# Expert loop of a two-layer gated network: rows marked three experts ahead, SiLU product kept in PSUM, low part of the down weight on VectorE

## The chip, the cores and the metric

One core of a Trainium2 chip. The metric is the device time of the whole program in microseconds (us); less is better. Before the change it is 2899.19 us, the median of three runs (2895.27 to 2901.91).

## What is computed

Four residual blocks run one after another on 1,024 tokens of width 512 (2 sequences of 512): a cross attention, a causal attention with a mixture of experts behind it, a second cross attention, and a quantised feed-forward. The change is in the mixture of experts of the second block, and nowhere else:

```python
logits = h @ wg                                   # 16 experts
topv, topi = jax.lax.top_k(logits, 4)             # 4 of them for each token
gate = jax.nn.softmax(topv, -1)
weights = jnp.zeros_like(logits).at[bidx, sidx, topi].set(gate)
a = silu(einsum('bsd,edh->bseh', h, w1)) * einsum('bsd,edh->bseh', h, w3)
y = einsum('bseh,ehd->bsed', a, w2)
moe = einsum('bsed,bse->bsd', y, weights)
return x + moe
```

w1, w3 and w2 (called gate, up and down weight here) are 512 x 512 for each expert.

## The kernel before

All matrix products of this stage are made of three products of fp32r halves: each operand is split in a high part (a copy to fp32r) and a low part (what the copy lost), and high x high, low x high and high x low are added up (`ACCURATE`). So each weight of 1 MB is loaded into one of two raw buffers `e_raw` by SP (L1751), copied to its high part by ACT (L1774, function `high`), and its low part is made by POOL as raw minus high (L1808, function `low`). The semaphore `s_lo` counts the low parts, three for each expert; SP's next load into a raw buffer waits for it.

The stage has two versions, chosen at run time by the count of the fullest expert. The one that runs here (functions `few_*`) gives each expert at most CAP = 320 tokens, in CT = 3 tiles of 128 places. The other (`every_*`) is compiled but not entered. For expert e, in the program's order on each engine:

- **PE** (`few_tensor`, L2142 on): gate and up product of the four chunks m of the hidden width, 24 matmuls of 320 columns each (L2154) into `GU[m % 2]`; then `order(e+2)`: 24 small matmuls (L2125) that multiply the marks of expert e+2 with the token table and so give the list of its tokens; then `turn(e+1)`: transposes of the gathered rows of the next expert (L2135), two chunks before and two behind the first tile of the down product; and the down product, 12 matmuls of 512 columns for each of three row tiles (L2172) into the two banks `Y`.
- **ACT** (`few_scalar`): high part of w2, which waits until the last down product of the expert before is done (there is one w2 buffer); per chunk SiLU (L1954) and `part_high` (L1943), the high part of the activation; high part of the next w1 behind chunk 1, of the next w3 behind chunk 3; then the high parts of the next expert's tokens (L1934).
- **DVE** (`few_vector`, L2084 on): per chunk the product of SiLU and up (L2095) into the SBUF buffer `act32`, then some of the marks (L2043), then `part_low` (L2089), the low part of the activation. Behind the chunks `targets` and `listed` (some small operations on the lists), the low parts of the next tokens (L2071), and the eviction of each row tile, scaled by the gate (L2104).
- **POOL** (`few_gpsimd`): gather of the rows of expert e+1 (three indirect DMAs, L1985), then the three scatter-adds of expert e-1 into `y_sum` (L1996), and between them the low parts of w2, of the next w1 and of the next w3. A scatter-add waits (`s_sum`) until the one before it has landed. Ahead of each of them stands a one-element operation (L1995, L1983).

A mark is a 128 x 384 comparison: for one tile of 128 tokens, which of the 384 places of the expert its token takes. There are eight for each expert, written into the single buffer `e_mine`, and `mark(e)` waits until `order(e-1)` has read it. Where they stand is set by two lines:

```python
MARKS = (0, 3, 6, NT, NT)                       # NT = 8
mark(e + 2, range(MARKS[m], MARKS[m + 1]))      # in chunk m, between product and part_low
```

PE's `order(e+2)` waits for all eight (`s_mine`). The first two experts are written out, the other fourteen are a loop over pairs.

Of the kernel before, what the change touches and what calls it, by code (L numbers as in the profile page):

```python
# [7 lines left out]
P = 128  # L8
BANK = 512
# [39 lines left out]
def program(nc, a, out):  # L49
    ctx = ExitStack()  # L50
    with ctx:
# [1158 lines left out]
        CAP = T * TOPK // NE * 5 // 4  # L1210
        CT = -(-CAP // P)
        PLACES = CT * P
        place = sb("m_place", [P, NE + 2, NT])
        crowded = sb("m_crowded", [P, 1], I32)
        moe = {}
        h_rows = nc.dram_tensor("h_rows", (T, D), F32, kind="Internal").ap()
# [490 lines left out]
        def experts():  # L1707
# [6 lines left out]
            w2 = [sb(f"e_w2{i}", [P, HC, D], F32R) for i in range(2)]  # L1714
            silu = [sb(f"e_silu{i}", [P, BANK]) for i in range(2)]
            act32 = [sb(f"e_act{i}", [P, BANK]) for i in range(2)]
            carry = sb("e_carry", [P, 2])
            aT0 = [sb(f"e_aT0{i}", [P, HC, BANK], F32R) for i in range(2)]
            with ExitStack() as every_only:
                aT = [aT0, [every_only.enter_context(nc.sbuf_tensor(f"e_aT1{i}", [P, HC, BANK], F32R)) for i in range(2)]]  # L1720
            with ExitStack() as few_only:
# [12 lines left out]
            s_in = [sem(f"e_in{i}") for i in range(2)]  # L1734
            s_mine, s_list, s_id, s_xt, s_xh, s_xl, s_got, s_tg = [
                sem(f"e_{n}") for n in ("mine", "list", "id", "xt", "xh", "xl", "got", "tg")]
            s_up = sem("e_up")
            s_freed = sem("e_freed")
            s_back = [sem(f"e_back{i}") for i in range(2)]
            s_sum = sem("e_sum")  # L1740
# [162 lines left out]
            def few_sync(sp):  # L1903
                def body(i, s, last):
                    e = i * 2 + s
                    for k, kind in enumerate(("w2", "w1", "w3")):
                        if not (last and k):
                            sp.wait_ge(s_lo, 3 * e + k + 1)
                            load(sp, 3 * s + k, e + (1 if k else 0), kind)

                sp.dma_start(count_up[:, :], a["c_count_up"].partition_broadcast(P)).then_inc(s_up, 16)
                load(sp, 0, 0, "w1")
                load(sp, 1, 0, "w3")
                with sp.Fori(0, NE // 2 - 1) as i:
                    for s in range(2):
                        body(i, s, False)
                body(NE // 2 - 1, 0, False)
                body(NE // 2 - 1, 1, True)
                sp.wait_ge(s_sum, 16 * CT * NE)
                for k in range(2):  # L1920
                    sp.dma_start(y3[:, k * NT // 2:(k + 1) * NT // 2, :],
                                 y_sum[k * T // 2:(k + 1) * T // 2, :].rearrange("(t p) d -> p t d", p=P)).then_inc(s_back[k], 16)

            def few_scalar(act):
# [13 lines left out]
                def body(i, s, last):  # L1938
                    e = i * 2 + s

                    def part_high(m):
                        act.wait_ge(s_a, HC * (e + 1) + m + 1)
                        act.activation(aT0[0][:, m, 0:CAP], act32[m % 2][:, 0:CAP], ACT.Copy).then_inc(s_ah, 1)  # L1943

                    def next_high(w, k):

                        n = 3 * s + k
                        high(act, w[1 - s][0], 16 * (3 * i + 1 + n // 2 + 1), n % 2)

                    act.wait_ge(s_y, CT * (e + 1))  # L1950
                    high(act, w2[0], 16 * (3 * i + (1 if s == 0 else 3)) + (0 if s else 16), s)
                    for m in range(HC):
                        act.wait_ge(s_gu, HC * (e + 1) + m + 1)
                        act.activation(silu[m % 2][:, 0:CAP], GU[m % 2][:, 0:CAP], ACT.Silu).then_inc(s_sg, 1)  # L1954
                        part_high(m)
                        if not last and m == 1:
                            next_high(w1, m)
                    if not last:
                        next_high(w3, 2)
                    tokens(e + 1, 1 - s)  # L1960
# [12 lines left out]
            def few_gpsimd(pool):  # L1973
# [3 lines left out]
                def gather(e, s):  # L1977

                    pool.wait_ge(s_id, LIST * e + LIST)
                    if not (isinstance(e, int) and e == 0):  # L1980
                        pool.wait_ge(s_xt, KC * e)

                    pool.tensor_tensor(carry[:, s:s + 1], eps[:, 0:1], eps[:, 0:1], ALU.mult)  # L1983
                    for r in range(CT):
                        pool.indirect_dma_start(rows[:, r, :], None, h_rows,  # L1985
                                                bass.IndirectOffsetOnAxis(ap=ids[s][:, r:r + 1], axis=0)).then_inc(s_got, 16)
# [17 lines left out]
                def body(i, s, first, last):  # L2004
                    e = i * 2 + s
                    gather(e + 1, 1 - s)
                    if not first:
                        scatter(e - 1, 1 - s, 0)
                    low(pool, w2, 3 * e + 3, s)
                    if not first:  # L2010
                        scatter(e - 1, 1 - s, 1)
                    if not last:
                        low(pool, w1[1 - s], 3 * e + 4, (3 * s + 1) % 2)
                    if not first:
                        scatter(e - 1, 1 - s, 2)
                    if not last:
                        low(pool, w3[1 - s], 3 * e + 5, (3 * s + 2) % 2)
# [12 lines left out]
            def few_vector(dve):  # L2030
# [48 lines left out]
                listed(1, 1)  # L2079
                tokens(0, 0)  # L2080

                MARKS = (0, 3, 6, NT, NT)

                def body(i, s):  # L2084
                    e = i * 2 + s

                    def part_low(m):
                        dve.wait_ge(s_ah, HC * e + m + 1)
                        dve.tensor_tensor(aT0[1][:, m, 0:CAP], act32[m % 2][:, 0:CAP], aT0[0][:, m, 0:CAP].bitcast(F32),  # L2089
                                          ALU.subtract).then_inc(s_al, 1)  # L2090

                    for m in range(HC):
                        dve.wait_ge(s_al, HC * e + m + 1)
                        dve.wait_ge(s_sg, HC * e + m + 1)
                        dve.tensor_tensor(act32[m % 2][:, 0:CAP], silu[m % 2][:, 0:CAP], GU[m % 2][:, BANK:BANK + CAP],  # L2095
                                          ALU.mult).then_inc(s_a, 1)
                        mark(e + 2, range(MARKS[m], MARKS[m + 1]))
                        part_low(m)
                    targets(e, s)
                    listed(e + 2, s)  # L2100
# [1 line left out]
                    for r in range(CT):  # L2102
                        dve.wait_ge(s_y, CT * (e + 1) + r + 1)
                        dve.tensor_scalar(y3[:, CT * s + r, :], Y[(r + 1) % 2][:, :], share[s][:, r:r + 1], None, ALU.mult).then_inc(s_yd, 1)  # L2104

                for s in range(2):
                    body(0, s)
# [5 lines left out]
            def few_tensor(pe):  # L2113
# [28 lines left out]

                def body(i, s):
                    e = i * 2 + s
                    pe.wait_ge(s_lo, 3 * e + 1)
                    pe.wait_ge(s_xl, KC * (e + 1))
                    for m in range(HC):
                        pe.wait_ge(s_a, HC * (e + 1) + m - 1)
                        for j, w in enumerate((w1[s], w3[s])):
                            if j and m == 0:  # L2150
                                pe.wait_ge(s_lo, 3 * e + 2)
                            for n, (x0, x1) in enumerate(ACCURATE):
                                for c in range(KC):
                                    mm = pe.matmul(GU[m % 2][:, j * BANK:j * BANK + CAP], w[x0][:, c, m * P:(m + 1) * P],  # L2154
# [4 lines left out]
                    order(e + 2)  # L2159

                    turn(e + 1, range(2))
                    pe.wait_ge(s_lo, 3 * e + 3)
                    pe.wait_ge(s_al, HC * (e + 1) + 1)
                    for r in range(CT):
                        pe.wait_ge(s_yd, CT * (e + 1) + max(r - 1, 0))
# [851 lines left out]
```

## Time and profile before

| | |
|---|---|
| median of 3 runs | 2899.19 us (2895.27 to 2901.91) |
| profiled execution, its own time | 2897.7 us |
| its span | 2895.9 us |
| PE busy | 2411.6 us (83%) |
| DVE busy | 1781.1 us (62%) |
| ACT busy | 1482.8 us (51%) |
| POOL busy | 1160.3 us (40%) |
| granted PE clock, mean | 0.934 |
| gate and up products (L2154), PE busy | 230.4 us |
| low parts of weights (L1808), POOL busy | 222.0 us for 48, 4627 ns each |

The expert stage runs from about 1708 to 2200 us of the span. Shares are of the span of one profiled execution; a granted clock of 1 is 2.4 GHz and 0.5 is 1.2 GHz. Operations are named by line, engine and the tiles that they write and read.

### The profile page before, as it was taken

The page shows a single profiled execution, that of the slowest core. Times are in us where ns is not written, and L with a number is a line of the kernel's source. Part 1 is how long each engine was busy: PE and PEld are TensorE (multiplying, and loading weights), DVE is VectorE, ACT ScalarE, POOL GpSimd, SP SyncE. Part 2 cuts the span into 40 slices and gives each one's busy share as a digit, 9 for nine tenths or more (in the row PEclk, how much of TensorE's full clock was granted, in tenths as well). Part 3 has the DMA queues.
Part 4 walks back from the last instruction along what each step waited for, and adds up shares of the span by engine and source line. Part 5 has one row for each costly group of instructions (what it writes and reads, how often), then busy time and mean ns, then how long its engine had stood idle before and what let it go on. Part 6 is the DMA issues. An engine that isn't in the chain of part 4 may idle for free. (4 is left out here: it accounts for less than half of the span.)

```text
span 2895.9 us, 46257 instructions
## 1 busy us (share of the span) xinstructions
PE 2411.6 (83%) x14790; PEld 2004.4 (69%) x14790; DVE 1781.1 (62%) x3865; ACT 1482.8 (51%) x3037; POOL 1160.3 (40%) x1561
## 2 busy tenths in 40 slices
PE   6999999999975998889885749999994698899365
PEld 3778787878864888888874538888883576677232
DVE  2555555555544666666665626565655787788576
ACT  3444444444435666666663443344332776777543
POOL 0222222222222444444442467787771544444000
PEclk9999999999996999999996969999997899999778
DMA  3000000000001000000003465665556332321100
GB/s 110 19 12 18 7 18 11 14 11 18 0 1 40 19 19 18 18 18 18 8 11 122 156 227 151 174 167 165 162 148 167 90 93 63 95 76 66 76 8 22
DMA packets 123653, 190.90 MB, mean 66 GB/s; under 512 B 18273, under 2 KB 66657, under 8 KB 121761
## 3 DMA queue, kind: packets, MB, share of 16 engines
q1 hardware_dynamic: 111408, 161.69, 18.3%
q0 software_dynamic: 10992, 25.96, 4.0%
q10 hardware_dynamic: 1152, 2.10, 0.3%
q8 instruction: 41, 0.67, 0.1%
q14 instruction: 60, 0.48, 0.1%
HBM read 143.58 MB, written 46.14 MB: 66 GB/s over the span
## 5 line engine op out<-in xcount | busy, mean ns | idle before, releaser
L435 ACT ACTIVATE x_p<-x_p,x_least 128x1024 f32<-128x1024 f32 x128 | 147.3, 1151 | 307.5 <-DVE x_least L391 307.5
L1808 POOL TENSOR_TENSOR e_w<-e_raw,e_w 128x2048 fp32r<-128x2048 f32 x48 | 222.0, 4627 | 70.5 <-ACT e_w L1774 70.4
L469 POOL TENSOR_TENSOR x_carry<-x_rtotal 128x1 f32<-128x1 f32 x128 | 24.7, 193 | 560.0 <-DVE x_rtotal L368 560.0
L375 DVE TENSOR_TENSOR x_pT<-pair,x_pT 128x512 fp32r<-128x512 f32 x256 | 164.4, 684 | 122.4 <-ACT x_pT L454 122.4
L2154 PE MATMUL pair<-m_h,e_w 128*128 128x320 f32 x1536 | 230.4, 311 | 1.1 <-DVE m_h L2071 1.1
L2154 PEld LDWEIGHTS pair<-m_h,e_w 128*128 128x128 f32 x1536 | 229.0, 190 | 2.9 <-issue 1.5
L537 PE MATMUL pair<-x_pT,x_v 128*128 128x256 f32 x1536 | 209.6, 293 | 9.2 <-DVE x_pT L375 9.2
L537 PEld LDWEIGHTS pair<-x_pT,x_v 128*128 128x128 f32 x1536 | 194.0, 194 | 26.3 <-issue 18.3
L565 PE MATMUL pair<-x_kT,x_qT 128*128 128x512 f32 x768 | 207.1, 405 | 0.0
L993 ACT ACTIVATE s_p<-s_p,s_least 128x128 f32<-128x128 f32 (+3 forms) x256 | 143.6, 561 | 123.4 <-DVE s_least L903 123.4
L2497 DVE TENSOR_REDUCE z_most<-pair 128x1 f32<-128x1008 f32 x128 | 154.0, 1203 | 73.4 <-PE pair L2607 51.2
L1131 PE MATMUL pair<-s_pT,s_v 128*128 128x256 f32 (+1 forms) x1152 | 158.3, 284 | 47.6 <-DVE s_pT L880 47.6
L1131 PEld LDWEIGHTS pair<-s_pT,s_v 128*128 128x128 f32 x1152 | 152.7, 195 | 60.1 <-issue 30.8
L2519 ACT ACTIVATE z_pT<-pair 128x512 fp32r<-128x512 f32 x256 | 141.7, 601 | 95.7 <-PE pair L2568 82.8
L1053 POOL TENSOR_TENSOR s_carry<-s_rtotal 128x1 f32<-128x1 f32 x256 | 49.6, 194 | 346.8 <-DVE s_rtotal L874 346.5
L2568 PE MATMUL pair<-ident,z_p 128*128 128x128 f32 x1024 | 144.6, 281 | 51.0 <-DVE z_pT L2490 49.9
L2533 ACT ACTIVATE z_p<-pair,z_most 128x1008 f32<-128x1008 f32 (+1 forms) x256 | 174.3, 696 | 12.5 <-DVE z_most L2498 12.5
L2568 PEld LDWEIGHTS pair<-ident,z_p 128*128 128x128 f32 x1024 | 117.1, 142 | 90.4 <-DVE z_pT L2490 61.8
L880 DVE TENSOR_TENSOR s_pT<-pair,s_pT 128x128 fp32r<-128x128 f32 (+3 forms) x256 | 124.7, 487 | 81.1 <-ACT s_pT L979 81.1
L2553 POOL TENSOR_SCALAR z_p<-z_p,z_rtotal 128x1008 f32<-128x1008 f32 (+1 forms) x256 | 174.6, 695 | 0.0
L2490 DVE TENSOR_TENSOR z_pT<-pair,z_pT 128x512 fp32r<-128x512 f32 x256 | 163.1, 679 | 4.5 <-ACT z_pT L2519 3.8
L454 ACT ACTIVATE x_pT<-pair 128x512 fp32r<-128x512 f32 x256 | 138.3, 594 | 45.0 <-PE pair L523 45.0
(336 smaller groups left out, 6189.9 us busy)
## 6 DMA issues: line engine op xcount, KB each, us to landing
e_raw<-in_L_ffn_w SPq DMA_DIRECT2D x48, 1024.0 KB
z_v<-z_vst SPq DMA_DIRECT2D x16, 768.0 KB, 3.6
z_kS<-z_k SPq DMA_DIRECT2D x24, 512.0 KB, 10.6
z_vS<-z_v SPq DMA_DIRECT2D x8, 1536.0 KB, 6.5
f_raw<-in_L_ffn_w SPq DMA_DIRECT2D x2, 4096.0 KB, 13.4
z_qS<-z_q SPq DMA_DIRECT2D x24, 256.0 KB, 4.5
s_wraw<-in_L_ffn_wq SPq DMA_DIRECT2D x9, 512.0 KB, 4.4
x_wq<-in_L_xattn_Wq SPq DMA_DIRECT2D x8, 512.0 KB, 3.6
```

The costliest lines, as they stand in the source:

```text
L375: dve.tensor_tensor(pT[1][:, keys, q * P:(q + 1) * P], TR[j][:, :].rearrange("p (k n) -> p k n", n=P), pT[0][:, keys, q * P:(q + 1) * P].b ...
L435: act.activation(p[n][:, :], p[n][:, :], ACT.Exp, scale=-1.0, bias=least[:, n:n + 1], accum_out=total[:, n:n + 1]).then_inc(s_ex, 1)
L537: mm = pe.matmul(OB[:, cols], v[x0][b][:, k, :], pT[x1][:, k, cols], start=(half == 0 and n == 0 and k == 0), stop=(half == 1 and n == 2 a ...
L565: mm = pe.matmul(SC[n % 2][:, j * BANK:(j + 1) * BANK], qT[x0][b][n // QT][:, n % QT * P:(n % QT + 1) * P], kT[x1][b][:, j * BANK:(j + 1) ...
L1131: mm = pe.matmul(OB[:, cols], v[b][:, k, first:first + 2, :].rearrange("p k d -> p (k d)"), pT[x1][:, k, cols], start=(i % 2 == 0 and half ...
L1808: pool.tensor_tensor(dst[1][:, :, :], raw[parity][:, :, :], dst[0][:, :, :].bitcast(F32), ALU.subtract).then_inc(s_lo, 1)
L2154: mm = pe.matmul(GU[m % 2][:, j * BANK:j * BANK + CAP], w[x0][:, c, m * P:(m + 1) * P], XS[s][x1][:, c, :], start=(n == 0 and c == 0), sto ...
L2490: dve.tensor_tensor(pT[1][:, k, cols], TR[i][:, :].rearrange("p (k n) -> p k n", n=P), pT[0][:, k, cols].bitcast(F32), ALU.subtract).then_ ...
L2497: dve.tensor_reduce(most[:, w, 0:1], SC[n % 2][:, 0:MAIN], AX.X, ALU.max, negate=True)
L2533: act.activation(p[w][:, cols], SC[n % 2][:, cols], ACT.Exp, bias=most[:, w, k:k + 1], accum_out=total[:, w, k:k + 1]).then_inc(s_ex, 1)
L2553: pool.tensor_scalar(p[w][:, cols], p[w][:, cols], rtotal[:, w, k:k + 1], 1.0, ALU.mult, ALU.mult).then_inc(s_pn, 1)
L2568: mm = pe.transpose(TR[i][:, k * P:(k + 1) * P], p[n % RING][:, kk * P:(kk + 1) * P], ident[:, :])
```

## The change

It does three things, all in the `few_*` functions.

1. **Marks.** They leave the four chunks. `mark(e+3)` now stands behind the row evictions of expert e, three behind the first, three behind the second and two behind the third; `mark(2)` is made whole ahead of the first expert. `place` gets one more column of zeros for it.
2. **Product.** The product of SiLU and up is written back into `GU` (PSUM) over the gate half, and `part_high` and `part_low` read it there. PE's wait ahead of a chunk is now for `part_low` of the chunk two before (`s_al`), where it was for the product (`s_a`).
3. **Low part of w2.** It moves from POOL to DVE, to the head of an expert's work, with a semaphore of its own (`s_lo2`). On POOL the first two scatter-adds then stand next to each other.

```diff
@@ -1210,7 +1210,7 @@
         CAP = T * TOPK // NE * 5 // 4
         CT = -(-CAP // P)
         PLACES = CT * P
-        place = sb("m_place", [P, NE + 2, NT])
+        place = sb("m_place", [P, NE + 3, NT])
         crowded = sb("m_crowded", [P, 1], I32)
         moe = {}
         h_rows = nc.dram_tensor("h_rows", (T, D), F32, kind="Internal").ap()
@@ -1714,7 +1714,6 @@
             w2 = [sb(f"e_w2{i}", [P, HC, D], F32R) for i in range(2)]
             silu = [sb(f"e_silu{i}", [P, BANK]) for i in range(2)]
             act32 = [sb(f"e_act{i}", [P, BANK]) for i in range(2)]
-            carry = sb("e_carry", [P, 2])
             aT0 = [sb(f"e_aT0{i}", [P, HC, BANK], F32R) for i in range(2)]
             with ExitStack() as every_only:
                 aT = [aT0, [every_only.enter_context(nc.sbuf_tensor(f"e_aT1{i}", [P, HC, BANK], F32R)) for i in range(2)]]
@@ -1734,7 +1733,7 @@
             s_in = [sem(f"e_in{i}") for i in range(2)]
             s_mine, s_list, s_id, s_xt, s_xh, s_xl, s_got, s_tg = [
                 sem(f"e_{n}") for n in ("mine", "list", "id", "xt", "xh", "xl", "got", "tg")]
-            s_up = sem("e_up")
+            s_up, s_lo2 = sem("e_up"), sem("e_lo2")
             s_freed = sem("e_freed")
             s_back = [sem(f"e_back{i}") for i in range(2)]
             s_sum = sem("e_sum")
@@ -1905,7 +1904,10 @@
                     e = i * 2 + s
                     for k, kind in enumerate(("w2", "w1", "w3")):
                         if not (last and k):
-                            sp.wait_ge(s_lo, 3 * e + k + 1)
+                            if k < 2:
+                                sp.wait_ge(s_lo, 2 * e + k + 1)
+                            else:
+                                sp.wait_ge(s_lo2, e + 1)
                             load(sp, 3 * s + k, e + (1 if k else 0), kind)
 
                 sp.dma_start(count_up[:, :], a["c_count_up"].partition_broadcast(P)).then_inc(s_up, 16)
@@ -1940,7 +1942,7 @@
 
                     def part_high(m):
                         act.wait_ge(s_a, HC * (e + 1) + m + 1)
-                        act.activation(aT0[0][:, m, 0:CAP], act32[m % 2][:, 0:CAP], ACT.Copy).then_inc(s_ah, 1)
+                        act.activation(aT0[0][:, m, 0:CAP], GU[m % 2][:, 0:CAP], ACT.Copy).then_inc(s_ah, 1)
 
                     def next_high(w, k):
 
@@ -1980,7 +1982,7 @@
                     if not (isinstance(e, int) and e == 0):
                         pool.wait_ge(s_xt, KC * e)
 
-                    pool.tensor_tensor(carry[:, s:s + 1], eps[:, 0:1], eps[:, 0:1], ALU.mult)
+                    pool.tensor_tensor(scrap[:, 58 + s:59 + s], eps[:, 0:1], eps[:, 0:1], ALU.mult)
                     for r in range(CT):
                         pool.indirect_dma_start(rows[:, r, :], None, h_rows,
                                                 bass.IndirectOffsetOnAxis(ap=ids[s][:, r:r + 1], axis=0)).then_inc(s_got, 16)
@@ -2006,7 +2008,6 @@
                     gather(e + 1, 1 - s)
                     if not first:
                         scatter(e - 1, 1 - s, 0)
-                    low(pool, w2, 3 * e + 3, s)
                     if not first:
                         scatter(e - 1, 1 - s, 1)
                     if not last:
@@ -2079,22 +2080,23 @@
                 listed(1, 1)
                 tokens(0, 0)
 
-                MARKS = (0, 3, 6, NT, NT)
+                MARKS = (0, 3, 6, NT)
+                mark(2)
 
                 def body(i, s):
                     e = i * 2 + s
+                    dve.wait_ge(s_hi, 3 * e + 3)
+                    dve.tensor_tensor(w2[1][:, :, :], raw[s][:, :, :], w2[0][:, :, :].bitcast(F32), ALU.subtract).then_inc(s_lo2, 1)
 
                     def part_low(m):
                         dve.wait_ge(s_ah, HC * e + m + 1)
-                        dve.tensor_tensor(aT0[1][:, m, 0:CAP], act32[m % 2][:, 0:CAP], aT0[0][:, m, 0:CAP].bitcast(F32),
+                        dve.tensor_tensor(aT0[1][:, m, 0:CAP], GU[m % 2][:, 0:CAP], aT0[0][:, m, 0:CAP].bitcast(F32),
                                           ALU.subtract).then_inc(s_al, 1)
 
                     for m in range(HC):
-                        dve.wait_ge(s_al, HC * e + m + 1)
                         dve.wait_ge(s_sg, HC * e + m + 1)
-                        dve.tensor_tensor(act32[m % 2][:, 0:CAP], silu[m % 2][:, 0:CAP], GU[m % 2][:, BANK:BANK + CAP],
+                        dve.tensor_tensor(GU[m % 2][:, 0:CAP], silu[m % 2][:, 0:CAP], GU[m % 2][:, BANK:BANK + CAP],
                                           ALU.mult).then_inc(s_a, 1)
-                        mark(e + 2, range(MARKS[m], MARKS[m + 1]))
                         part_low(m)
                     targets(e, s)
                     listed(e + 2, s)
@@ -2102,6 +2104,7 @@
                     for r in range(CT):
                         dve.wait_ge(s_y, CT * (e + 1) + r + 1)
                         dve.tensor_scalar(y3[:, CT * s + r, :], Y[(r + 1) % 2][:, :], share[s][:, r:r + 1], None, ALU.mult).then_inc(s_yd, 1)
+                        mark(e + 3, range(MARKS[r], MARKS[r + 1]))
 
                 for s in range(2):
                     body(0, s)
@@ -2142,13 +2145,13 @@
 
                 def body(i, s):
                     e = i * 2 + s
-                    pe.wait_ge(s_lo, 3 * e + 1)
+                    pe.wait_ge(s_lo, 2 * e + 1)
                     pe.wait_ge(s_xl, KC * (e + 1))
                     for m in range(HC):
-                        pe.wait_ge(s_a, HC * (e + 1) + m - 1)
+                        pe.wait_ge(s_al, HC * e + m + 1)
                         for j, w in enumerate((w1[s], w3[s])):
                             if j and m == 0:
-                                pe.wait_ge(s_lo, 3 * e + 2)
+                                pe.wait_ge(s_lo, 2 * e + 2)
                             for n, (x0, x1) in enumerate(ACCURATE):
                                 for c in range(KC):
                                     mm = pe.matmul(GU[m % 2][:, j * BANK:j * BANK + CAP], w[x0][:, c, m * P:(m + 1) * P],
@@ -2159,7 +2162,7 @@
                     order(e + 2)
 
                     turn(e + 1, range(2))
-                    pe.wait_ge(s_lo, 3 * e + 3)
+                    pe.wait_ge(s_lo2, e + 1)
                     pe.wait_ge(s_al, HC * (e + 1) + 1)
                     for r in range(CT):
                         pe.wait_ge(s_yd, CT * (e + 1) + max(r - 1, 0))
```

On DVE, from the evictions of expert 0 into the chunks of expert 1 (written-out part; `y` is the evicted tile, `e_mine` the marks, `e_act` the product in SBUF, `e_aT` the low part of the activation). Before:

```order
L2104 TENSOR_SCALAR y<-pair,e_share 128x512 x3
L2095 TENSOR_TENSOR e_act<-e_silu,pair 128x320
L2043 TENSOR_SCALAR e_mine<-e_count_up,m_place 128x384 x3
L2089 TENSOR_TENSOR e_aT<-e_act,e_aT 128x320
L2095 TENSOR_TENSOR e_act<-e_silu,pair 128x320
L2043 TENSOR_SCALAR e_mine<-e_count_up,m_place 128x384 x3
L2089 TENSOR_TENSOR e_aT<-e_act,e_aT 128x320
L2095 TENSOR_TENSOR e_act<-e_silu,pair 128x320
L2043 TENSOR_SCALAR e_mine<-e_count_up,m_place 128x384 x2
L2089 TENSOR_TENSOR e_aT<-e_act,e_aT 128x320
```

and now (line numbers of the changed kernel):

```order
L2106 TENSOR_SCALAR y<-pair,e_share 128x512
L2044 TENSOR_SCALAR e_mine<-e_count_up,m_place 128x384 x3
L2106 TENSOR_SCALAR y<-pair,e_share 128x512
L2044 TENSOR_SCALAR e_mine<-e_count_up,m_place 128x384 x3
L2106 TENSOR_SCALAR y<-pair,e_share 128x512
L2044 TENSOR_SCALAR e_mine<-e_count_up,m_place 128x384 x2
L2089 TENSOR_TENSOR e_w<-e_raw,e_w 128x2048
L2098 TENSOR_TENSOR pair<-e_silu,pair 128x320
L2093 TENSOR_TENSOR e_aT<-pair,e_aT 128x320
L2098 TENSOR_TENSOR pair<-e_silu,pair 128x320
L2093 TENSOR_TENSOR e_aT<-pair,e_aT 128x320
```

The marks have gone from between the products to between the evictions, and one operation of 2,048 columns stands ahead of the first product.

On POOL, the work of expert 1 (`y_sum<-y` is a scatter-add, `e_rows` the gather, `e_w` a low part). Before:

```order
L1985 DMA e_rows<-h_rows,e_ids 128x512 x3
L1995 TENSOR_TENSOR scrap<-eps 128x1
L1996 DMA y_sum<-y,e_target 1408x512
L1808 TENSOR_TENSOR e_w<-e_raw,e_w 128x2048
L1995 TENSOR_TENSOR scrap<-eps 128x1
L1996 DMA y_sum<-y,e_target 1408x512
L1808 TENSOR_TENSOR e_w<-e_raw,e_w 128x2048
L1995 TENSOR_TENSOR scrap<-eps 128x1
L1996 DMA y_sum<-y,e_target 1408x512
L1808 TENSOR_TENSOR e_w<-e_raw,e_w 128x2048
```

and now:

```order
L1987 DMA e_rows<-h_rows,e_ids 128x512 x3
L1997 TENSOR_TENSOR scrap<-eps 128x1
L1998 DMA y_sum<-y,e_target 1408x512
L1997 TENSOR_TENSOR scrap<-eps 128x1
L1998 DMA y_sum<-y,e_target 1408x512
L1807 TENSOR_TENSOR e_w<-e_raw,e_w 128x2048
L1997 TENSOR_TENSOR scrap<-eps 128x1
L1998 DMA y_sum<-y,e_target 1408x512
L1807 TENSOR_TENSOR e_w<-e_raw,e_w 128x2048
```

One of three low parts has left, the one between the first and the second scatter-add.

## Rows read from the trace of the kernel before

**Rows 1.** Stretches: PE, PEld, DVE, ACT, POOL busy; clock, DMA share, GB/s.

```profile
1960.80:1989.57 28.77, 26.74 (x170) 24.40 (x168) 16.79 (x32) 10.47 (x15) 22.37 (x14) 0.94 0.59 163
2102.47:2129.72 27.25, 25.33 (x169) 23.16 (x168) 16.62 (x32) 10.63 (x16) 21.25 (x12) 1.00 0.58 153
2157.33:2182.00 24.67, 24.67 (x170) 22.54 (x168) 13.34 (x33) 6.98 (x13) 12.42 (x10) 1.00 0.40 60
1730.69:2157.33 426.64, 395.33 (x2520) 360.53 (x2521) 251.66 (x479) 167.09 (x240) 335.62 (x194) 0.96 0.59 166
```

**Rows 2.** The chain of waits around experts 14 and 15: start, length, what.

```profile
2144.50 1.16 issue
...
2146.23 1.49 PE pair L2125 x24
...
2151.23 0.66 PE pair L2135 x6
2151.88 5.61 PE pair L2172 x24
2157.49 14.08 PE pair L2154 x96
2171.58 0.60 PE pair L2125 x24
2172.17 0.72 PE pair L2135 x6
2172.89 2.81 PE pair L2172 x12
```

**Rows 3.** The timeline of the expert that PE begins at 1961.03 us.

```profile
1961.34 1.92 ACT L1774 ACTIVATE e_w<-e_raw 128x2048 fp32r<-128x2048 f32 x1 [3.76 <-PE pair L2172]
...
1972.03 4.57 POOL L1808 TENSOR_TENSOR e_w<-e_raw,e_w 128x2048 fp32r<-128x2048 f32 x1 [1.99 <-ACT e_w L1774]
...
1972.77 4.38 DVE L2043 TENSOR_SCALAR e_mine<-e_count_up,m_place 128x384 bf16<-128x384 f32 x2
...
1978.36 1.90 ACT L1774 ACTIVATE e_w<-e_raw 128x2048 fp32r<-128x2048 f32 x1
...
1980.61 0.89 DVE L2071 TENSOR_TENSOR m_h<-pair,m_h 128x320 fp32r<-128x320 f32 x2 [0.38 <-ACT m_h L1934]
...
1984.90 0.18 POOL L1983 TENSOR_TENSOR e_carry<-eps 128x1 f32<-128x1 f32 x1
...
1988.82 0.21 POOL L1995 TENSOR_TENSOR scrap<-eps 128x1 f32<-128x1 f32 x1
```

**Rows 4.** The marks' own line: shortest, median and longest in ns.

```profile
L2043 DVE TENSOR_SCALAR e_mine<-e_count_up,m_place x144: 405/410/4057, 1713.3 to 2169.4; 128x384 bf16<-128x384 f32 x144
```

**Rows 5.** PE behind a wait for marks: stretch, busy (matmuls), granted clock, DMA share, GB/s.

```profile
1948.00:1955.00 7.00, 6.58 (x45) 0.76 0.71 187
```

**Rows 6.** The one DVE line elsewhere with the shape and form of the moved operation.

```profile
L1377 DVE TENSOR_TENSOR z_cT<-z_ctxraw,z_cT x2: 2285/2288/2291, 1574.1 to 1576.3; 128x2048 fp32r<-128x2048 f32 x2
```

**Rows 7.** The products' line on DVE: shortest, median and longest in ns.

```profile
L2095 DVE TENSOR_TENSOR e_act<-e_silu,pair x64: 473/486/490, 1737.4 to 2172.2; 128x320 f32<-128x320 f32 x64
```

**Rows 8.** The scatter-adds' line on POOL, and their time to landing.

```profile
L1996 POOL DMA_INDIRECT y_sum<-y,e_target x48: 1562/1621/1681, 1762.4 to 2189.6; - x48
...
DMA to landing us min/median/max: 4.5/6.4/8.0
```

**Rows 9.** The timeline ahead of the first expert.

```profile
1717.28 2.71 DVE L2043 TENSOR_SCALAR e_mine<-e_count_up,m_place 128x384 bf16<-128x384 f32 x8
...
1718.34 1.77 POOL L1985 DMA_INDIRECT e_rows<-h_rows,e_ids  x1 [0.60 <-issue]
1720.42 0.97 POOL L1985 DMA_INDIRECT e_rows<-h_rows,e_ids  x1 [0.30 <-issue]
```

**Rows 10.** The chain at the head of the first expert, and behind the last.

```profile
1730.69 6.17 PE pair L2154 x24
...
2178.51 4.74 DMA y_sum<-y,e_target
```

## The prediction

> **What bounds the kernel now.** I read the busy shares first, then the chain of waits, then the expert stage by stretches and its timeline. In the expert stage PE works nearly all the time. The first fifteen experts take 426.64 us, 28.44 each, and PE is busy for 395.33 of them: 31.3 us idle, 2.09 for each expert [rows 1]. Read single: 28.77 us with 26.74 busy, 27.25 with 25.33 busy, and the last expert 24.67 without a gap [rows 1]. The chain names the gap: behind the last gate and up product it goes over DVE's marks (1.16 us of issue, a mark) to the small matmuls of `order`, which take 1.49 us there and 0.60 in the last expert [rows 2]. The reader is to see two things in that pair of rows. PE stands in front of marks that are not ready. And when it doesn't stand, the same 24 matmuls take 0.89 us less: I read this as their address registers, which are then set while earlier matmuls still run.
>
> Why the marks are late: one takes 0.41 us in the median and up to 4.06 [rows 4]. POOL begins a low part at 1972.03 and ends it at 1976.60; the pair of marks begins at 1972.77 and is over at 1977.15, so the first stood until POOL was through [rows 3]. `part_low`, the fourth product and all behind them queue after it on DVE. The last expert has no next weights, POOL makes no low part in its later chunks, and there is no gap: it is the picture of the changed kernel, inside the old one.
>
> A third cost hangs on the gap: the granted clock. Over 7 us behind one wait it is 0.76 [rows 5], so some 3.4 us at the lower level, 1.2 GHz, where the expert at 27.25 us shows 1.00 throughout [rows 1]. What went before is a PE idle of about 2 us. It explains most of the 1.5 us between the two kinds of expert.
>
> **The change, part by part.**
>
> *Marks to the evictions.* This removes the wait (2.09), the slow `order` (0.89) and, if the clock holds, the drops. The pieces of an expert without them are 14.08 gate and up, 0.60 order, 0.72 and 0.66 transposes, 2.81 and 5.61 down product [rows 2]: 24.48 us. Against 28.44 that is 3.96, of which 2.98 are the first two terms and 0.98 the clock, 0.18 of it the slow head of the first expert (24 matmuls in 6.17 us [rows 10], for a quarter of 14.08 = 3.52), which stays. At their new place the marks meet POOL's low part of w3. That begins when ACT has made the high part, about 3.4 us behind the last gate product, 17.5 from PE's start, and takes 4.57 [rows 3]: until 22.1. The first eviction is over at 14.1+0.6+0.7+2.8+0.75 = 19.0, so its three marks stand until 22.1 and end about 23.2, and the second eviction comes 1.3 us late. Nobody on the path waits for it: the third tile needs the first eviction, the list the second one 16 us later. All eight marks are over about 1.5 us into the next expert. Cost nothing; cover gone, each eviction held up costs PE what it is late. The eight extra marks ahead of the first expert take 2.7 us [rows 9] beside PE's 6.17 [rows 10]; nothing.
>
> The Trainium skill (SBUF — State Buffer, "Who interferes with whom") has the rule behind this: a DVE operation in a two-port mode and a GpSimd operation exclude each other for the whole instruction. The trace agrees with the 4.06 us above. By that rule the new place is no safer than the old one, only less waited for.
>
> *Tokens.* With the gap gone a shorter one may open. Behind the last gate product SiLU, product and high part end at about 1.6 us; ACT then makes w3's high part (1.90), and DVE's token parts begin 2.25 behind its start [rows 3], at 3.75, the first ready at 4.2. PE wants it at 0.60+0.72+2.81 = 4.13 [rows 2]. Bounds 0.1 and 0.5; I take 0.35 for each expert.
>
> *Product in PSUM.* No row shows DVE writing PSUM. Below, it costs what the write to SBUF costs, 0.486 [rows 7]; above, twice that, which would delay the tokens by 0.49 and cost 7 us in all. Reading it from PSUM is priced by the token parts, two in 0.89 [rows 3], as now. I take nothing more: both are one pass over 320 columns. PE's new wait, for `part_low` two chunks back, has cover: see next.
>
> *Low part of w2 on DVE.* The same form took 2.29 [rows 6]. The high part ends 2.2 us into the expert [rows 3], so DVE is busy to 4.6. SiLU of chunk 0 is ready at 4.1; the product moves to 5.1, `part_low` ends at 6.3, and PE wants it at 7.05 (two quarters of 14.08). 0.8 us of cover, then each us more is paid once per expert. SP's load of the next w3 starts 2.3 us sooner, as the raw buffer comes free sooner.
>
> *POOL.* It loses 4.6 us per expert but also the work that hid the landing of the first scatter-add. Its own round is now gather 3.92 [rows 3], three one-element operations of 0.4, two landings L, the third issue 1.62 [rows 8], and the low part of w3 4.6; w1's hides in the second landing. That is 11.3 + 2L: 20.3, 24.1 or 27.3 us for L of 4.5, 6.4 or 8.0 [rows 8]. PE's round is 24.83. The likeliest value leaves PE the bound, by 0.7.
>
> **The sum.** 15 x (24.48 + 0.35) + 2.65 = 375.1 us for 426.6, so 51.5 less; the last expert and what follows, three scatter-adds landing one after another (4.74 for one [rows 10]), stay. The profiled execution takes 2897.7, and the median is 1.5 above it: 2899.2 - 51.5 = **2847.7 us**.
>
> **The rivals.**
> (a) *POOL's round becomes the bound.* For it: descriptors made beside marks took 1.77 us, where the next took 0.97 [rows 9], and marks now run beside the gather, so up to two of three issues may grow by 0.8 and the round reaches 25.7 at L = 6.4; the loads come closer together, too. Then 15 x 0.9 = 13 us more: 2861. The same page of the Trainium skill says that a GpSimd-queue DMA starves for descriptors while DVE is in such a mode; by that rule this case is the likelier. Against it: DVE's marks stand behind the low part for part of that time. With L at 8.0 it is 27.3, 37 us more: 2885.
> (b) *DVE is late at the head of the expert* (w2's low part behind held marks, or slower): 2 us of delay less 0.8 of cover is 1.2 x 15 = 18 us: 2866. Against it: the marks end 0.8 us before the high part does.
> (c) *The change doesn't do all it says*: the clock falls without the gap as well. Then 0.8 x 15 = 12 us more: 2860.
> (d) *Slower than before.* POOL's chain of landings, the first scatter-add now bare, exceeds 28.44 us. It decides at L = 8.6. At 9.0 it is 29.3: 13 us slower than before, 2912. Against it: the longest of 48 landings took 8.0 [rows 8].
>
> **How the numbers follow.** Forecast 0.65, (a) small 0.13 and large 0.04, (b) 0.06, (c) 0.07, (d) 0.03, and 0.02 for a gain that comes out at nothing for a reason not seen. The forecast's own bounds are 24.58 per expert (2844) and, with the dear PSUM write, 25.3 (2855); the three runs reach 3.9 us below their median, and that goes below: 2840. (a) small, (b) and (c) reach to 2866, so the range is 2840 to 2867 and leaves out the large (a), (d) and the ends. Faster by over 0.2%, about what a measurement of this kernel can tell from none: 0.65+0.13+0.04+0.06+0.07 = 0.95; within 0.2%: 0.02; slower: 0.03.
>
> **What would show it.** Right: experts 24.6 to 25.1 us apart, `order` at 0.60 us, no PE wait for marks, clock 1.00 from the second expert on, marks up to about 3.5 us long behind the first eviction. Wrong: PE waiting for `e_w` or for rows (POOL's round), `part_low` late for the third chunk (DVE), or half-clock stretches without a gap ahead of them. The forecast falls if POOL is found without idle time and the experts are over 25.3 us apart.

## The result, and the profile after

The changed kernel takes **2845.32 us** (median of 5 runs, 2844.33 to 2848.66) for 2899.28 of the kernel before, run on the same chip: a ratio of 0.9814, 95% interval 0.9803 to 0.9825, 54 us less. Forecast were 2847.7 us and a range of 2840 to 2867. The profiled execution took 2844.89 us, its span is 2843.1.

Stretches of the changed kernel; columns as in [rows 1]: experts 1 to 14, the last one, and one of the fourteen.

```profile
1756.96:2102.86 345.90, 343.19 (x2354) 316.15 (x2354) 206.64 (x462) 155.31 (x223) 248.20 (x169) 1.00 0.71 191
2102.86:2127.20 24.34, 24.34 (x169) 22.47 (x168) 13.86 (x33) 6.84 (x13) 8.24 (x10) 1.00 0.42 66
1979.33:2004.04 24.71, 24.54 (x171) 22.59 (x170) 14.79 (x33) 10.44 (x15) 17.73 (x13) 1.00 0.70 188
```

Fourteen experts in 345.90 us are 24.71 each, PE idle for 0.19 of them, the clock at 1.00: it answers to the row of fifteen experts in [rows 1] (28.44, idle 2.09, clock 0.96). From PE's first matmul of expert 0 (1729.82) to that of expert 15 (2102.86) it is 373.0 us for 426.6, so 53.6 us less; the two profiled executions differ by 52.8 (2897.7 and 2844.9). The rest of the program adds up to 0.8 us more: 0.9 less ahead of the loop, 1.7 more from expert 15 on.

The chain of waits of the changed kernel through one expert:

```profile
1979.33 14.11 PE pair L2157 x96
...
1993.47 0.45 ACT e_silu L1956
1993.94 0.51 DVE pair L2098
...
1994.80 1.91 ACT e_w L1773
1996.70 0.33 ACT m_h L1936
1997.06 0.50 DVE m_h L2072
...
1997.70 0.85 PE pair L2138 x6
1998.55 5.49 PE pair L2175 x24
2004.04 14.11 PE pair L2157 x96
```

No mark is in it. In the kernel before every expert of the loop has one on the chain, between the rows of [rows 2] this one:

```profile
2145.66 0.42 DVE e_mine L2043
```

The reader is to see what took their place: behind the last gate product the chain leaves PE for the last product, then w3's high part (1.91 us) and the next tokens, and comes back to PE's transposes at 1997.70, 0.17 us after PE had run dry. This is the short token wait that was expected.

The timeline of the same expert:

```profile
1981.43 2.29 DVE L2089 TENSOR_TENSOR e_w<-e_raw,e_w 128x2048 fp32r<-128x2048 f32 x1 [0.55 <-ACT e_w L1773]
...
1986.03 0.18 POOL L1997 TENSOR_TENSOR scrap<-eps 128x1 f32<-128x1 f32 x1 [3.32 <-DMA y_sum<-y,e_target]
...
1993.27 0.76 PE L2128 MATMUL pair<-e_token,e_mine 128*128 x24
...
1996.79 4.61 POOL L1807 TENSOR_TENSOR e_w<-e_raw,e_w 128x2048 fp32r<-128x2048 f32 x1 [0.57 <-ACT e_w L1773]
...
1999.53 0.74 DVE L2106 TENSOR_SCALAR y<-pair,e_share 128x512 f32<-128x512 f32 x1
2000.19 2.09 DVE L2044 TENSOR_SCALAR e_mine<-e_count_up,m_place 128x384 bf16<-128x384 f32 x3
```

`order` begins with the end of the gate products (x24 in 0.76; the timeline counts its overlap with them, the chain has 0.60 for such a group). The moved low part takes 2.29 us, as its like in [rows 6]. POOL waits 3.3 us for the first scatter-add to land, 47.8 us in all fourteen experts. All of it is slack, as a run below shows. The marks behind the first eviction are still held by POOL's low part (1996.79 to 2001.40) and go on when it ends.

The marks, the product written to PSUM, and the landings, to be laid beside [rows 4], [rows 7] and [rows 8]:

```profile
L2044 DVE TENSOR_SCALAR e_mine<-e_count_up,m_place x152: 401/410/1529, 1712.5 to 2128.2; 128x384 bf16<-128x384 f32 x152
```

```profile
L2098 DVE TENSOR_TENSOR pair<-e_silu,pair x64: 487/495/497, 1736.3 to 2117.5; 128x320 f32<-128x320 f32 x64
```

```profile
DMA to landing us min/median/max: 4.6/5.3/7.1
```

The longest mark takes 1.53 us, where it took 4.06; a product costs 0.01 us more for going to PSUM; a landing takes 5.3 us in the median, not 6.4.

### The profile page after: what moved, and what is told of

It reads as the page before. It is cut to its first block and busy times, and to the rows that moved or that the text cites. A ratio compares the mean times of both kernels' runs of the same rounds, so it can differ in the third digit from the quotient of the medians.

```text
span 2843.1 us, 46195 instructions
## 1 busy us (share of the span) xinstructions
PE 2385.3 (84%) x14782; PEld 1985.4 (70%) x14790; DVE 1755.0 (62%) x3889; ACT 1482.6 (52%) x3037; POOL 1086.3 (38%) x1545
## 5 line engine op out<-in xcount | busy, mean ns | idle before, releaser
L1807 POOL TENSOR_TENSOR e_w<-e_raw,e_w 128x2048 fp32r<-128x2048 f32 x32 | 146.7, 4587 | 39.6 <-ACT e_w L1773 39.6
```

Source lines behind the costliest of these rows:

```text
L1807: pool.tensor_tensor(dst[1][:, :, :], raw[parity][:, :, :], dst[0][:, :, :].bitcast(F32), ALU.subtract).then_inc(s_lo, 1)
```

## The experiments

Ten more kernels ran. The distance of experts is that of experts 1 to 14, from PE's first matmul of one to that of the next; idle is PE's per expert; both come from a stretch as above. The time of the kernel before on the same chip stands beside each.

| run | median us | before | ratio (95%) | expert | idle | clock |
|---|---|---|---|---|---|---|
| before | | | 1 | 28.16 | 2.09 | 0.97 |
| the change | 2845.3 | 2899.3 | 0.9814 (0.9803 to 0.9825) | 24.71 | 0.19 | 1.00 |
| marks only | 2868.1 | 2902.2 | 0.9883 (0.9867 to 0.9900) | 26.10 | 1.37 | 1.00 |
| marks and PSUM product | 2850.0 | 2902.2 | 0.9821 (0.9805 to 0.9838) | 24.71 | 0.19 | 1.00 |
| marks and low part on DVE | 2855.5 | 2902.2 | 0.9841 (0.9824 to 0.9857) | 25.50 | 0.75 | 1.00 |
| all but the marks | 2902.6 | 2902.2 | 1.0002 (0.9992 to 1.0012) | 28.42 | 1.60 | 0.93 |
| before, other table | 2883.4 | 2900.8 | 0.9937 (0.9920 to 0.9953) | 27.19 | 2.01 | 0.99 |
| all but the marks, other table | 2844.7 | 2900.8 | 0.9808 (0.9791 to 0.9824) | 24.71 | 0.19 | 1.00 |
| the change, a wait put in | 2916.6 | 2899.6 | 1.0062 (1.0046 to 1.0077) | 29.12 | 2.71 | 0.95 |
| the same, fixed address | 2888.5 | 2899.6 | 0.9962 (0.9946 to 0.9977) | 27.29 | 2.13 | 0.97 |
| the change, free scatter-adds | 2839.6 | 2899.6 | 0.9798 (0.9785 to 0.9811) | 24.70 | 0.19 | 1.00 |
| the same, tokens first | 2832.2 | 2899.6 | 0.9769 (0.9755 to 0.9782) | 24.31 | 0.00 | 1.00 |

### Which part brings the gain

**Marks only.** The changed kernel with the product in `act32` and w2's low part on POOL, both as before. The cut shows where each went; the two readers of the product and the waits that belong to it are set back too.

```diff
-                    dve.wait_ge(s_hi, 3 * e + 3)
-                    dve.tensor_tensor(w2[1][:, :, :], raw[s][:, :, :], w2[0][:, :, :].bitcast(F32), ALU.subtract).then_inc(s_lo2, 1)
...
+                    pool.wait_ge(s_hi, 3 * e + 3)
+                    pool.tensor_tensor(w2[1][:, :, :], raw[s][:, :, :], w2[0][:, :, :].bitcast(F32), ALU.subtract).then_inc(s_lo2, 1)
...
-                        dve.tensor_tensor(GU[m % 2][:, 0:CAP], silu[m % 2][:, 0:CAP], GU[m % 2][:, BANK:BANK + CAP],
+                        dve.tensor_tensor(act32[m % 2][:, 0:CAP], silu[m % 2][:, 0:CAP], GU[m % 2][:, BANK:BANK + CAP],
```

> The changed kernel with its other two parts undone: the product goes to SBUF again and w2's low part is on POOL again; only the marks have moved. My theory: PE's wait for the marks goes, but part_low, a DVE operation with two SBUF inputs, is shut out by POOL's low parts, which the marks took the blame for before: part_low of chunks 0 and 2 ends with POOL's operation, the fourth product and the tokens come 1 to 2 us late and PE waits for the tokens; experts 25.5 to 27 us apart, 2858 to 2880 us. Rival 1 (the marks are everything): experts 24.7 us apart, 2845 us. Rival 2 (POOL's round with three low parts is the bound without the slack of the wait): PE waits for e_w, over 2880 us.

Measured: 2868.1 us, experts 26.10 apart, both inside what the theory said. The timeline around the third chunk shows why:

```profile
1930.62 4.57 POOL L1807 TENSOR_TENSOR e_w<-e_raw,e_w 128x2048 fp32r<-128x2048 f32 x1 [1.02 <-ACT e_w L1773]
...
1931.98 3.56 DVE L2093 TENSOR_TENSOR e_aT<-e_act,e_aT 128x320 fp32r<-128x320 f32 x1 [0.54 <-ACT e_aT L1945]
...
1935.46 0.47 DVE L2099 TENSOR_TENSOR e_act<-e_silu,pair 128x320 f32<-128x320 f32 x1
```

`part_low`, 0.49 us when free, begins at 1931.98 and ends at 1935.54, just behind POOL's operation (1935.19). The next product stands behind it on DVE. PE waits twice in each expert: 0.76 us at the down product, which needs this `part_low`, and 0.61 for the tokens. It never waits for `e_w`. Rivals 1 and 2 fall: it isn't all in the marks, and POOL is not the bound.

**Marks and PSUM product**: the first two lines of the diff above undone on DVE, put on POOL; the product stays in PSUM.

> Marks moved and product in PSUM, but w2's low part on POOL as before. My theory: part_low has one SBUF input now and is never shut out, and POOL's round of some 23.7 us fits under 24.7, so this is as fast as the whole change: 2845 us, within 3 us. Rival (the low part on DVE is what is needed, since POOL has no room for it): POOL without idle time, experts 25 to 26 us apart, 2850 to 2865 us.

Measured: experts 24.71 apart, ratio 0.9821, inside the interval of the whole change. The 2850.0 us are 2 above the range that was expected; this chip gives the kernel before 2902.2. `part_low` in this run, and in the run with the marks only:

```profile
L2093 DVE TENSOR_TENSOR e_aT<-pair,e_aT x64: 491/492/493, 1743.3 to 2124.5; 128x320 fp32r<-128x320 f32 x64
```

```profile
L2093 DVE TENSOR_TENSOR e_aT<-e_act,e_aT x64: 491/494/3572, 1742.6 to 2144.0; 128x320 fp32r<-128x320 f32 x64
```

The longest is 0.493 us with one input in PSUM and 3.57 with both in SBUF; POOL makes its three low parts for each expert in both.

**Marks and low part on DVE**: the product in SBUF again (last pair of the diff).

> Marks moved and w2's low part on DVE, but the product in SBUF as before. My theory: part_low of chunk 2 meets POOL's low part of w1 and ends with it, about 3 us late; the fourth product and the tokens follow 0.5 to 1.5 us late; experts 25.2 to 26.2 us apart, 2853 to 2868 us. Rival (an operation with two SBUF inputs is not shut out): part_low stays at 0.49 us each and the time is 2845 us.

Measured: experts 25.50 us apart, 2855.5 us in all, ratio 0.9841, as expected. That is 0.79 us per expert behind the change: `part_low` still meets w1's low part (3.30 us at the longest). So with the marks gone, the PSUM product is what frees DVE; moving w2's low part then adds nothing that shows, and without the PSUM product it is worth 0.60 us per expert (26.10 to 25.50).

**All but the marks**: `mark(e + 2, ...)` back in the chunks with the table (0, 3, 6, NT, NT), the rest of the change in place.

> The marks back in the chunks, two experts ahead, with the product in PSUM and w2's low part on DVE. My theory: the last marks still meet POOL's low part of w1 and PE waits for them as before; at most the first chunk's marks get through sooner: 2885 to 2900 us. Rival (POOL's third low part was what held the marks, so moving it alone brings the gain): PE's wait goes, 2850 to 2865 us.

Measured: 2902.6 us, ratio 1.0002. That is slower than the 2885 to 2900 expected: the theory was right that the wait would stay, and wrong that something would be gained. The rival falls. Its chain has the old wait:

```profile
1947.43 0.45 ACT e_silu L1956
...
1948.30 4.07 DVE e_mine L2044 x2
...
1952.51 1.48 PE pair L2127 x24
```

PE's idle time fell from 2.09 to 1.60 us per expert, but its busy time rose from 26.07 to 26.81, with the granted clock at 0.93 for 0.97. That gave it back.

### Is it the place of the marks, or what they meet there?

**Before, other table**: one line of the kernel before.

```diff
-                MARKS = (0, 3, 6, NT, NT)
+                MARKS = (0, 4, NT, NT, NT)
```

> The kernel before with one line changed: the numbers that place the marks are (0, 4, 8, 8, 8), so that four stand in chunk 0, four in chunk 1 and none in chunk 2. My theory: what held the last marks was POOL's low part of w1, which begins behind chunk 1; the ones in chunk 1 are then made ahead of it, PE's wait for marks goes, and part_low of chunk 2 (two SBUF inputs) stands behind that low part in their place, as in the run where only the marks were moved: experts 25.8 to 26.6 us apart, ratio 0.985 to 0.991, 2860 to 2872 us. Rival (marks between the products cost PE a wait wherever they stand): experts 28 us apart or more, ratio 0.998 to 1.005.

Measured: 0.9937, between the theories' ranges: a miss. The wait for marks is gone, as the theory has it. But the four marks in chunk 0 are now held by POOL's low part of w2 (4.51 us; four unheld ones take 1.40), and `part_low` of chunk 2 by that of w1. Two places of the timeline:

```profile
1957.55 4.51 DVE L2043 TENSOR_SCALAR e_mine<-e_count_up,m_place 128x384 bf16<-128x384 f32 x4
```

```profile
1965.27 4.54 POOL L1808 TENSOR_TENSOR e_w<-e_raw,e_w 128x2048 fp32r<-128x2048 f32 x1 [2.40 <-ACT e_w L1774]
1966.69 3.47 DVE L2089 TENSOR_TENSOR e_aT<-e_act,e_aT 128x320 fp32r<-128x320 f32 x1 [0.61 <-ACT e_aT L1943]
...
1970.26 3.04 PE L2172 MATMUL pair<-e_w,e_aT 128*128 128x512 f32 x12 [1.82 <-POOL e_w L1808]
```

The down product waits 1.8 us. The profile names POOL's operation, but that was over at 1969.81; what the program waits for there is this `part_low`, over at 1970.16. The expectation had left out the first of the two: behind the held marks chunk 1 is late, with it ACT's high part of w1 and POOL's low part, and so `part_low` of chunk 2 ends later. The down product waits 1.57 us per expert for it, 0.76 in the run with the marks only.

**All but the marks, other table**: the same line in the kernel of 1.0002.

> The same table in the kernel that has the marks in the chunks, the product in PSUM and w2's low part on DVE (without the table 1.000 of the time before). My theory: no mark and no part_low meets a low part of POOL; part_low of chunk 0 comes at about 7.0 us where PE wants it at 7.05, so there may be a small wait there: experts 24.7 to 25.2 us apart, ratio 0.981 to 0.984. Rival (marks must leave the chunks): over 0.99.

Measured: 0.9808, experts 24.71 apart, no mark longer than 0.64 us. So the marks need not leave the chunks. What they must not meet is POOL's low parts; with w2's on DVE, chunks 0 and 1 are free of them. This table was not run with w2's low part left on POOL and the product in PSUM.

### What a wait on PE costs

**The change, a wait put in**, and **the same, fixed address**. The first cut is in both, the second in the latter alone; it gives the loop's experts the shares of expert 2, so its output is not the layer's, while the amount of work is the same.

```diff
                     pe.wait_ge(s_yd, CT * (e + 1) - 1)
+                    pe.wait_ge(s_al, HC * (e + 1) + 2)
                     order(e + 2)
```

```diff
-                            tok = moe["token"][:, e, t, :] if isinstance(e, int) else (
-                                moe["token"][:, bass.ds(e, 1), t, :].rearrange("p e k -> p (e k)"))
+                            tok = moe["token"][:, e if isinstance(e, int) else 2, t, :]
```

> The changed kernel with one wait more on PE: ahead of order it waits for the low part of the fourth chunk (about 2.1 us behind the last gate product), which it would wait for later anyway. My theory: the wait of about 2.1 us in 16 experts brings with it the slow order (1.49 for 0.60 us) and half-clock stretches, less 0.3 us of token wait that it swallows: 3.3 to 3.6 us per expert, 2895 to 2905 us. Rival (the wait alone costs, the other two terms are something else): 1.8 us per expert, 2874 us.

> As the run with the added wait, but order inside the loop reads the token table at a fixed expert (2), so that its 24 matmuls need no address register; the shares of the loop's experts are then those of expert 2, the amount of work is the same. If the slow order is its registers being set behind the wait: order takes 0.6 to 0.8 us and the time is 10 to 14 us below the run with the wait alone. If it is an effect of the idle time or the clock on the matmuls: order stays near 1.49 us and the time is the same.

Measured: 2916.6 and 2888.5 us. The chain behind the wait, first with the address in a register, then with the fixed one:

```profile
1949.34 0.45 ACT e_silu L1956
...
1951.55 1.53 PE pair L2128 x24
1953.08 1.38 PE pair L2138 x6
1954.46 4.88 PE pair L2176 x12
```

```profile
1942.47 0.50 DVE e_aT L2093
...
1943.10 0.75 PE pair L2127 x24
1943.85 0.71 PE pair L2137 x6
1944.56 2.77 PE pair L2175 x12
```

With a fixed address `order` takes 0.75 to 0.80 us behind the same wait in all sixteen experts, with the register 1.45 to 1.53. The rows of the address registers show when they are set, in the run with the wait and in the changed kernel:

```profile
L2128 PEldq FUSED_REGOPS  x8: 46/46/51, 1951.4 to 1952.4; - x8
L2128 PEldq FUSED_REGOPS  x8: 46/46/65, 1990.8 to 1991.8; - x8
```

Behind the wait the eight are set from just ahead of the first matmul of `order` to past its middle (it runs from 1951.55 to 1953.08). Without the wait they are done 1.4 us before `order` begins (1993.27), and with the fixed address there are none. The clock is not the reason: in the kernel before `order` takes 1.46 to 1.49 us in the ten experts where its stretch has clock 1.00, and 1.48 to 1.52 in the five at 0.55 to 0.87. What is left between 0.76 and 0.60 I read as lost overlap: the timeline above shows 0.76 for an `order` without a wait too, and the chain counts 0.60 of it because it begins beside the last gate products.

Both expectations were too low in size. The wait costs 4.41 us per expert (29.12 for 24.71), not 3.3 to 3.6: idle 2.52 more, `order` 0.9 more, and about 1 us from stretches at a lower clock (0.95 in the mean), as the down product's 4.88 for 2.77, with 0.54 granted. The fixed address saves 28 us, not 10 to 14: 1.83 per expert, of which 0.72 are `order` (1.49 and 0.77 in the mean), 0.58 less idle, and the rest goes with the clock (0.97 for 0.95). How these hang together was not taken apart.

### What is left

**The change, free scatter-adds**:

```diff
-                    if not (isinstance(e, int) and e == 0 and r == 0):
-                        pool.wait_ge(s_sum, 16 * (CT * e + r))
+                    if r == 0 and not (isinstance(e, int) and e == 0):
+                        pool.wait_ge(s_sum, 16 * CT * e)
```

> The changed kernel, with the wait ahead of a scatter-add only at the first of an expert's three: the three write different rows (a token is once in an expert's list), so only those of the expert before must have landed. Behind the last expert the three were 5.5 us apart, each behind the landing of the one before; now about 2 us: 6 to 7 us less, 2838 to 2840 us. In the loop POOL gains slack, worth nothing if PE is the bound, as I hold. If POOL's round bounds in part (rival a of the prediction), the experts also come closer together than 24.71 us.

Measured: 2839.6 us, as expected, with experts 24.70 apart: only the end of the stage got shorter. From PE's start on expert 15 to the reload of `y_sum` it is 30.3 us for 36.7 (2103.77 to 2134.08, and 2102.86 to 2139.58). That the experts don't come closer shows POOL's round not to be the bound.

**The same, tokens first**: on ACT and on DVE `tokens(e + 1, 1 - s, range(2))` stands ahead of `next_high(w3, 2)` and of `targets`, the other two chunks where all four were.

> As the run without the waits between an expert's scatter-adds, and the first two chunks of the next tokens are made on ACT ahead of w3's high part and on DVE ahead of the small list operations. If the token wait (0.23 us over the pieces, 24.71 for 24.48) is the last one of PE: experts 24.45 to 24.5 us apart, 3 to 4 us below the other run, 2835 us. If w3's high part, now 0.9 us later, pushes POOL or the loads: no gain or a loss of up to 5 us.

Measured: 2832.2 us, the fastest of all, 0.9769. It is 7.4 us below the other run, not 3 to 4, and the experts are 24.31 apart, not 24.45 to 24.5: the pieces that the expectation subtracted from were 0.17 us too long. The chain through one expert is PE alone:

```profile
1952.85 14.10 PE pair L2159 x96
1966.94 0.60 PE pair L2130 x24
1967.54 0.71 PE pair L2140 x6
1968.26 2.79 PE pair L2177 x12
1971.05 0.66 PE pair L2140 x6
1971.70 5.46 PE pair L2177 x24
```

340.35 us busy in 340.35: 24.31 per expert. PE has no idle time left there and its clock is at 1.00, so only less work on PE would bring the experts closer.

## Why the prediction was right, point by point

- **The wait for marks, the slow `order`, the clock.** Right in kind and size for the change as a whole: idle 2.09 to 0.19, `order` 0.60 us, clock 1.00 from the second expert on. But the prediction gives all of it to the moving of the marks. Alone that brought 2.06 of the 3.45 us per expert, and 34 of the 54 us. That the slow `order` is its registers was read from one pair of rows; the fixed address showed it for 0.72 of the 0.89 us. That a wait brings stretches at a lower clock was shown by putting one in.
- **The undisturbed expert**, 24.48 us by its pieces: it is 24.31. The down products are a little shorter than in [rows 2] (5.46 and 2.79 for 5.61 and 2.81); why, stays open. **The token wait**, 0.35 taken: 24.71 less 24.31 is 0.40. Of this 0.19 is idle time, and as much is the transposes' lost overlap (0.85 for 0.66). The two errors partly cancel: 24.71 for 24.83, some 2 us in all, by which the forecast was high.
- **Marks at their new place.** Right that they are held by w3's low part and that it costs nothing. The step that timed them was wrong: it put the first eviction's end at 19.0 us behind PE's start, by the down product alone. On DVE the low parts of the third and fourth token chunk stand ahead of it, and it ends about 2 us later (2000.27 less 1979.33), so the marks are held less (2.09 us for the three, not 4; the longest is 1.53, not 3.5).
- **Product in PSUM.** Right that it adds next to nothing (0.01 us each), and wrong on what it is worth. The part on it priced only its own cost; that `part_low` would be held in the marks' place was not seen. It is this edit that keeps `part_low` out of POOL's way; without it 0.79 us per expert are lost, and 1.39 with w2's low part on POOL. The Trainium skill (SBUF — State Buffer, "Who interferes with whom") states this for a DVE operation with two SBUF inputs against a GpSimd operation that reads SBUF; the prediction used the rule for the marks and not for `part_low`. Here the runs agree with it: 3.57 us for 0.49 with both inputs in SBUF, 0.493 at most with one. The sum came out because the edit was in the change all the same: to that extent the hit is luck.
- **Low part of w2 on DVE.** 2.29 us, ends 4.4 us behind PE's start; right, and it was worth nothing by itself beside the PSUM product.
- **POOL's round** (rival a, and the decision point of rival d). A landing took 5.3 us, so the round is 11.3 + 10.6 = 21.9 us, and the runs without the waits left the experts where they were. The premise that issues beside marks are drawn out did not hold in the loop: beside them (1978.45, marks from 1978.15 on) an issue took 0.99 us, and none of the gather's took over 1.03.
- **Rivals b and c** did not come: `part_low` had its cover, and the clock did not fall once the gap was gone.

## What to carry to other kernels

When PE waits for a small operation, look at what that one meets on GpSimd before moving it: here a table of two numbers, with one operand kept in PSUM and w2's low part on DVE, did as much as moving the marks out of the chunks. A PE wait of 2 to 2.5 us in each round cost 3.5 to 4.4: the address registers were set behind it (0.9 us), and the clock was lower in part of what followed. And when one wait goes, work out which is next: it was the 0.40 us for the tokens, and a change of order on two engines took that as well.

## What was not expected of the hardware

- With the marks in their old place, the product in PSUM and w2's low part on DVE shortened PE's idle time from 2.09 to 1.60 us and came with a lower mean clock, 0.93 for 0.97; the time stayed the same (ratio 1.0002). The sum of idle time alone would have told of a gain. What lowered the clock was not taken apart.
- POOL is held by DVE as well. In the run with free scatter-adds POOL's one-element operation meets DVE's low part of w2 (two SBUF inputs) and ends with it. It takes 1.50 to 1.67 us there in each expert from the second on, with a median of 0.21 over all 48:

```profile
1982.36 2.35 DVE L2089 TENSOR_TENSOR e_w<-e_raw,e_w 128x2048 fp32r<-128x2048 f32 x1 [0.56 <-ACT e_w L1773]
1983.09 1.66 POOL L1997 TENSOR_TENSOR scrap<-eps 128x1 f32<-128x1 f32 x1
```

- In the changed kernel a gather's issue that began 0.05 us behind DVE's low part of w2 took three times as long as its neighbours:

```profile
1732.62 1.00 POOL L1987 DMA_INDIRECT e_rows<-h_rows,e_ids  x1 [0.30 <-issue]
1733.87 2.29 DVE L2089 TENSOR_TENSOR e_w<-e_raw,e_w 128x2048 fp32r<-128x2048 f32 x1 [0.42 <-ACT e_w L1773]
1733.92 3.06 POOL L1987 DMA_INDIRECT e_rows<-h_rows,e_ids  x1 [0.30 <-issue]
```

It is in the first expert alone, but in three traces: 2.95 us with free scatter-adds, where the issue began 0.16 us behind, and 3.09 with all but the marks and the other table (0.05 behind). Where it began 0.03 us ahead, or less than 0.02 behind (the wait put in, the fixed address, tokens first), it took 0.95. In the loop the scatter-add's issue comes 0.3 us ahead of that operation and takes its usual 1.6 us.
